# Two sixteen-head attentions: the values as stationary blocks, the denominators summed on GpSimd

## What is computed

```python
def _L0_xattn_ref(q, k, v, mask, Wq, bq, Wk, bk, Wv, bv, Wo, bo):
    B, N, DIM, H = (2, 512, 256, 16)
    qh = _split_heads(q @ Wq.T + bq)
    kh = _split_heads(k @ Wk.T + bk)
    vh = _split_heads(v @ Wv.T + bv)
    attn = jnp.einsum('bhqc,bhkc->bhqk', qh, kh) * SCALE
    attn = jnp.where(mask == 0, -jnp.inf, attn)
    attn = jax.nn.softmax(attn, axis=-1)
    out = jnp.einsum('bhqk,bhkc->bhqc', attn, vh)
    ...
    return out @ Wo.T + bo
...
x = x + jnp.tanh(g_xattn[0]) * _L0_xattn_ref(_layernorm(x, axis=-1), ctx_1024, ctx_1024, mask_1x1xSxS2_ik0, ...)
x = x + jnp.tanh(g_ffn[0]) * _L0_ffn_ref(_layernorm(x, axis=-1), ...)
...
x = x + jnp.tanh(g_xattn[3]) * _L3_xattn_ref(_layernorm(x, axis=-1), ctx_1024, ctx_1024, ...)
x = x + jnp.tanh(g_ffn[3]) * _L3_ffn_ref(_layernorm(x, axis=-1), ...)
```

## Time and profile before

| | us |
|---|---|
| median of three runs | 1044.92 (1043.39 to 1045.66) |
| the profiled execution's own time, its span | 1043.2 |
| first attention, its loop | about 29.4 to 139.5 |
| second attention, its loop | about 686.7 to 792.2 |
| TensorE busy over the span | 964.7 (92%) |
| VectorE busy | 603.3 (58%) |
| ScalarE busy | 489.0 (47%) |
| GpSimd busy | 287.8 (28%) |

### The profile page before, as it was taken

How to read it: one execution, slowest core, us unless ns; L and a number is a source line. 1 busy time by engine, 2 the same in 40 slices (tenths; PEclk the granted TensorE clock), 3 DMA queues, 4 the chain that set the end, 5 groups by cost and what they waited for, 6 DMA issues and landing times. The chain is left out here.

```text
span 1043.2 us, 18151 instructions
## 1 busy us (share of the span) xinstructions
PE 964.7 (92%) x6476; PEld 835.3 (80%) x6477; DVE 603.3 (58%) x1253; ACT 489.0 (47%) x744; POOL 287.8 (28%) x271
## 2 busy tenths in 40 slices
PE   6999999989999999877988889999998999999997
PEld 5778878878888888565777778887885799999996
DVE  5858769951223222689898999666776522222221
ACT  3654422111111111688785878255552556656561
POOL 2000000033444442280006112600000344444442
PEclk9999999999999999998999999999999999999999
DMA  9200040025667664011000010260115223322332
GB/s 295 69 1 22 21 143 21 21 77 166 181 181 210 182 168 91 15 41 41 1 1 2 1 41 2 99 231 21 41 42 171 83 45 50 48 45 48 51 45 31
DMA packets 62500, 79.38 MB, mean 76 GB/s; under 512 B 7340, under 2 KB 46855, under 8 KB 62439
## 3 DMA queue, kind: packets, MB, share of 16 engines
q1 hardware_dynamic: 48807, 59.95, 17.0%
q0 software_dynamic: 13632, 18.62, 10.2%
HBM read 60.73 MB, written 17.83 MB: 75 GB/s over the span
## 5 line engine op out<-in xcount | busy, mean ns | idle before, releaser
L3165 PEld LDWEIGHTS ps<-room,xn_sb 128*128 128x128 f32 x1248 | 145.6, 192 | 2.7 <-issue 0.8
L3165 PE MATMUL ps<-room,xn_sb 128*128 128x128 f32 x1248 | 146.3, 275 | 0.6 <-issue 0.6
L288 POOL TENSOR_TENSOR norm_vec<-norm_vec,powers 128x4 f32<-128x4 f32 (+2 forms) x27 | 28.9, 1071 | 360.7 <-DVE norm_vec L282 360.7
L3118 POOL DMA_INDIRECT out_x<-f_yo,f_give x39 | 62.0, 1589 | 110.5 <-DVE f_yo L3363 97.5
L3234 ACT ACTIVATE xn_sb<-w_L_ffn_w 128x1024 f32 x78 | 82.1, 1057 | 20.8 <-DVE f_te L3331 10.8
L3357 DVE TENSOR_TENSOR room<-room,ps 128x512 f32<-128x512 f32 x39 | 26.8, 687 | 109.5 <-PE ps L3165 109.5
L2857 DVE TENSOR_TENSOR room<-room,ps 128x1024 f32<-128x1024 f32 x24 | 29.3, 1219 | 104.0 <-issue 89.5
L2461 PE MATMUL ps<-b_room,room 128*128 128x256 f32 x384 | 85.6, 380 | 3.7 <-DVE room L2857 1.6
L2461 PEld LDWEIGHTS ps<-b_room,room 128*128 128x128 f32 x384 | 72.6, 190 | 14.1 <-issue 1.8
L2673 ACT ACTIVATE room<-ps 128x1024 f32<-128x1024 f32 x24 | 24.6, 1023 | 115.2 <-PE ps L2441 115.2
L2418 POOL DMA_INDIRECT acc_rows<-f_eo,f_idx x32 | 52.4, 1637 | 94.7 <-DVE f_eo L2883 50.9
(11 more groups left out here) (404 smaller groups left out, 2059.4 us busy)
## 6 DMA issues: line engine op xcount, KB each, us to landing
w_L_ffn_w<-in_L_ffn_w SPq DMA_DIRECT2D x24, 512.0 KB, 9.8
b_room<-in_L_ffn_Wg SPq DMA_DIRECT2D x16, 512.0 KB
b_room<-in_L_ffn_Wu SPq DMA_DIRECT2D x16, 512.0 KB
b_room<-in_L_ffn_Wd SPq DMA_DIRECT2D x16, 512.0 KB, 6.3
xn_rows<-xn_sb SPq DMA_DIRECT2D x8, 512.0 KB, 2.9
x_sb<-in_x SPq DMA_DIRECT2D x4, 512.0 KB, 6.4
xn_sb<-in_L_ffn_w SPq DMA_DIRECT2D x2, 1024.0 KB, 7.6
x_sb<-acc_rows SPq DMA_DIRECT2D x4, 512.0 KB, 5.9
```

The source lines that it names most:

```text
L3118: pool.indirect_dma_start(out_rows[:, :], bass.IndirectOffsetOnAxis(ap=give[:, j:j + 1], axis=0), yo[j % 2][:, :], None, compute_op=ALU.ad ...
L3165: m = pe.matmul(ps[:, banks[p], f * P:(f + 1) * P], wb[p][:, n, i, f * P:(f + 1) * P], xsT[p][:, i * P:(i + 1) * P], start=(i == 0), stop= ...
```

## The change

The heads are padded from 77 to 80 keys in the probabilities, so that 16 heads are 1280 columns, ten whole blocks, five for each half of the heads.

- `values`: the value blocks (128 keys x 32 columns, two heads) are stationary, the transposed probabilities move, 128 columns. Sixteen matmuls write four column groups of 32 columns each, first with the blocks of the two full rounds (early), then with the last round (late). What comes out is the output already transposed, so `turn_heads` and its copy on ScalarE are gone.
- Denominators: no column of ones is left in the value blocks. `denominators(n)` on GpSimd adds the exponentials 640, 320 and 160 wide; `inverse(n)` on VectorE, at the head of tile n, reduces the remaining 160 columns to 16 and takes the reciprocal; `widen(n)` on ScalarE spreads it over 256 columns, ahead of the tile's probability copies; TensorE transposes these two blocks in the third round; `normalise` is one multiply of the PSUM output by them.
- The third round is one copy of 512 columns: two blocks of probabilities and two of inverses.
- `project(n-1)` moves from the end of the tile to the place of `turn_heads`.
- `add_bias` moves from VectorE to GpSimd, behind the denominators.
- GpSimd's roots for the feed-forward are issued one by one inside the loop, a cast of lane numbers moves behind the loop, twenty selects of the opening become two. `place_values` has five matmuls in place of ten.

The core of the diff:

```diff
                     m.then_inc(s_ready, 1)
 
                 def turn(n, which):
+
                     pe.wait_ge(p_ready, n + 1)
                     for r in which:
-                        lo, hi = rounds[r]
                         if r == 2:
                             pe.wait_ge(pt_sb, 3 * n + 1)
-                        elif n:
-                            pe.wait_ge(pt_sb, 3 * n)
-                        for part in range(lo, hi):
-                            w = rows[part]
-                            m = pe.transpose(ps[0:w, 4 + r % 2, (part - lo) * P:(part - lo + 1) * P],
-                                             pr[:, n % 2, part * P:part * P + w], K.ident[:, :])
+                            for half in range(2):
+                                lo = half * HALF + 4 * P
+                                pe.transpose(ps[:, 4, half * P:(half + 1) * P], pr[:, n % 2, lo:lo + P], K.ident[:, :])
+                            pe.wait_ge(r_wide, n + 1)
+                            for k in range(KT):
+                                m = pe.transpose(ps[:, 4, (2 + k) * P:(3 + k) * P], wide[:, k * P:(k + 1) * P], K.ident[:, :])
+                        else:
+                            if n:
+                                pe.wait_ge(pt_sb, 3 * n)
+                            for q in range(4):
+                                lo = r * HALF + q * P
+                                m = pe.transpose(ps[:, 4 + r, q * P:(q + 1) * P], pr[:, n % 2, lo:lo + P], K.ident[:, :])
                         m.then_inc(pt_ps, 1)
 
                 def values(n):
+
+                    b = n // TB
                     if n:
-                        pe.wait_ge(on_ready, n)
-                    for r, (lo, hi) in enumerate(rounds):
-                        pe.wait_ge(pt_sb, 3 * n + r + 1)
-                        for part in range(lo, hi):
-                            w, h = rows[part], head0[part]
-                            m = pe.matmul(ps[:, 6, h * HV:(h + 3) * HV], pT[0:w, n % 2, part, :],
-                                          vblk[0:w, n // TB, part, :, :].rearrange("p j c -> p (j c)"),
-                                          start=(part == 0), stop=(part == NC - 1), skip_group_check=True)
+                        pe.wait_ge(oT_sb, n)
+                    for late in range(2):
+                        for half in range(2):
+                            pe.wait_ge(pt_sb, 3 * n + (3 if late else half + 1))
+                            for i in range(4):
+                                q = i + late
+                                m = pe.matmul(ps[i * RG:(i + 1) * RG, 6, half * P:(half + 1) * P],
+                                              vblk[:, q, 2 * b + half, 0 if late or i == 0 else 1, :], pT[:, n % 2, half if q < 4 else 2, q if q < 4 else half, :],
+                                              start=(half == 0 and not late), stop=bool(late), skip_group_check=True)
                     m.then_inc(o_ready, 1)
-
-                def turn_heads(n):
-                    pe.wait_ge(on_ready, n + 1)
-                    if n:
-                        pe.wait_ge(x_done, n)
-                    for k in range(KT):
-                        m = pe.transpose(ps[:, 7, k * P:(k + 1) * P], on[:, n % 2, k * P:(k + 1) * P], K.ident[:, :])
-                    m.then_inc(oT_ps, 1)
 
                 def project(n):
                     pe.wait_ge(oT_sb, n + 1)
                     if n == 0 and bo is not None:
                         pe.wait_ge(s_gbo, 1)
+                    if n:
+                        pe.wait_ge(x_done, n)
                     for k in range(KT):
-                        m = pe.matmul(ps[:, 7, D:2 * D], oT[:, k * P:(k + 1) * P], wo[:, k, :],
+                        m = pe.matmul(ps[:, 7, 0:D], oT[:, n % 2, k * P:(k + 1) * P], wo[:, k, :],
                                       start=(k == 0), stop=(k == KT - 1))
                     m.then_inc(y_ready, 1)
 
...
                         pe.wait_ge(q_sb, 4 * KT)
                     turn(n, (0, 1))
                     if n:
-                        turn_heads(n - 1)
+                        project(n - 1)
                     else:
                         scores(2)
-                        pe.wait_ge(s_vblk, 3)
+                        pe.wait_ge(s_vblk, PARTS + 1)
                         if bo is not None:
                             pe.wait_ge(*rest_in)
...
                         turn_second(n)
                     if ahead is not None:
                         ahead.tensor(pe, n, s_used)
-                    if n:
-                        project(n - 1)
-                unread(pe, K, 5, 2)
-                turn_heads(NT - 1)
-                unread(pe, K, 5, 1)
+                unread(pe, K, 5, 3)
                 project(NT - 1)
                 if ahead is not None:
                     ahead.tensor_end(pe)
...
                     act.wait_ge(p_in, n + 1)
                     if n >= 2:
                         act.wait_ge(pt_ps, 3 * (n - 1))
-                    act.activation(pr[:, n % 2, :], sm[:, n % 2, :], ACT.Exp).then_inc(p_ready, 1)
+                        act.wait_ge(s_den, 3 * (n - 2) + 1)
+                    act.activation(pr[:, n % 2, :].rearrange("p (h k) -> p h k", h=H)[:, :, 0:L],
+                                   sm[:, n % 2, :].rearrange("p (h k) -> p h k", h=H), ACT.Exp).then_inc(p_ready, 1)
+
+                def widen(n):
+
+                    act.wait_ge(r_den, n + 1)
+                    if n:
+                        act.wait_ge(pt_ps, 3 * n)
+                    act.activation(wide[:, :].rearrange("p (h d) -> p h d", h=H),
+                                   rden[:, n % 2, :].unsqueeze(2).broadcast_to([P, H, HD]), ACT.Copy).then_inc(r_wide, 1)
 
                 def copy_values():
                     act.wait_ge(s_vc, 1)
...
                     if n == TB - 2:
                         copy_queries(1, 0, (0, 1))
                         copy_queries(1, 1, (2, 3))
-                    for r, (lo, hi) in enumerate(rounds):
-                        if n and r == 2:
-                            act.wait_ge(oT_ps, n)
-                            act.activation(oT[:, :], ps[:, 7, 0:D], ACT.Copy).then_inc(oT_sb, 1)
+                    widen(n)
+                    for r in range(3):
                         act.wait_ge(pt_ps, 3 * n + r + 1)
                         if n >= 2 and r == 0:
                             act.wait_ge(o_ready, n - 1)
-                        if r < 2:
-                            act.activation(pT[:, n % 2, lo:hi, :].rearrange("p a b -> p (a b)"),
-                                           ps[:, 4 + r, :], ACT.Copy).then_inc(pt_sb, 1)
-                        else:
-                            act.activation(pT[:, n % 2, lo, :], ps[:, 4, 0:P], ACT.Copy)
-                            act.activation(pT[0:rows[-1], n % 2, lo + 1, :], ps[0:rows[-1], 4, P:2 * P],
-                                           ACT.Copy).then_inc(pt_sb, 1)
+                        if n >= 2 and r == 2:
+                            act.wait_ge(oT_sb, n - 1)
+                        act.activation(pT[:, n % 2, r, :, :].rearrange("p a b -> p (a b)"),
+                                       ps[:, 4 + r % 2, :], ACT.Copy).then_inc(pt_sb, 1)
                     if n in SECOND:
                         copy_second(n)
                     if n == 0:
...
+                def denominators(n):
+
+                    def add(src, w):
+                        lo = H * (LP - 2 * w)
+                        to = sm[:, n % 2, lo:lo + H * w].rearrange("p (h k) -> p h k", h=H)
+                        pool.tensor_tensor(to, src[:, :, 0:w], src[:, :, w:2 * w], ALU.add).then_inc(s_den, 1)
+                        return to
+
+                    pool.wait_ge(p_ready, n + 1)
+                    forty = add(pr[:, n % 2, :].rearrange("p (h k) -> p h k", h=H), LP // 2)
+                    pool.wait_ge(s_den, 3 * n + 1)
+                    twenty = add(forty, LP // 4)
+                    pool.wait_ge(s_den, 3 * n + 2)
+                    add(twenty, LP // 8)
+
+                def add_bias(n):
+                    if n == 0:
+                        pool.wait_ge(s_gbo, 2)
+                    elif n == 4:
+                        pool.wait_ge(norm.by_act, 4)
+                    elif n == TB:
+                        pool.wait_ge(norm.by_act, NT - 4)
+                    pool.tensor_tensor(K.x[:, n, :], K.x[:, n, :], gbo[:, :], ALU.add).then_inc(s_bias, 1)
+
+                if first:
...
                     dve.wait_ge(p_in, n + 1)
                     dve.sem_inc(s_used, 1)
 
+                def inverse(n):
+
+                    lo = H * (LP - LP // 4)
+                    dve.wait_ge(s_den, 3 * n + 3)
+                    dve.tensor_reduce(den[:, n % 2, :], sm[:, n % 2, lo:lo + H * LP // 8].rearrange("p (h k) -> p h k", h=H), AX.X,
+                                      ALU.add).then_inc(s_sum, 1)
```

(29 more changed lines are left out.)

130 lines of the change are left out of this document (69 added, 61 removed).

## The result

The changed kernel takes 1055.73 us (median of 4 runs, 1054.41 to 1056.91), beside 1045.01 for the kernel before in the same set of runs: a ratio of 1.010, 95% interval 1.0082 to 1.0118. It is 10.7 us slower; 1044.5 was forecast, with a range up to 1060 and a chance of 0.43 for slower. The time lies inside the range, but well outside the forecast's own 1040 to 1050, and the case that happened is none of those that were priced.

The account below looks back on a forecast made before the run. TensorE was taken as the bound, VectorE 0.5 us behind. Terms -1.15 + 1.35 - 1.6 - 1.2 + 3.0 - 0.8 = -0.4 took 1044.9 to 1044.5 us; range 1036 to 1060, the forecast's own 1040 to 1050.

Parts of the forecast that it names:

- What bounds the kernel now, and what TensorE gives back: Attention tiles: TensorE sets the pace, VectorE 0.5 us behind; values fall from 2.17 to 1.0 us.
- The rivals on that: Column groups in values: tile-shape switches cost +5 us, 1050, chance 0.07; groups do not overlap, +35, 1080, chance 0.04.
- The values cycle: Chain from inverse through widen, copies, transposes and values to multiply: 5.88 us per tile with rows; -1.15 first attention, +1.35 second.
- chain hidden: Faster rival: VectorE's front covers the chain from inverse to values, rows tiles take 5.77 us; 1037.5, chance 0.24.
- GpSimd: Denominator adds 2.8 us and bias 0.63 on GpSimd, 3.4 in a tile of 5.9; nothing waits for them: zero.
- The rival on GpSimd: Slower rival: GpSimd's adds double to 6.8 us a first-attention tile and become the bound past 5.9; 1058.5, chance 0.07.
- The last tiles and the end: Tiles 14 and 15 lengthen by 0.77 and 1.66 us, the end saves 0.9: net +1.5 an attention, +3.0.
- The turns: Turning tiles 7, 8, 11, 12 of the first attention go from 6.49 to 6.08 us; turns of tiles 1 to 4 unchanged.
- Project moved: Project no longer covers ScalarE's copy of the turns; turning tiles give -1.6 us in the first attention, -1.2 in the second.
- Prologue: Placing the values takes 2.0 us at most after 2.2 before; taken as -0.4 each, -0.8, bounds 0 and -1.
- The cast: GpSimd's moved cast of lane numbers lies beside other work: zero, at worst 2 us at the end.
- The clock: Slower rival: TensorE, busy 4.6 of 5.9 us, falls to 1.2 GHz; 1058 in ten tiles, over 1150 in all; chance 0.13.

Follow-up runs that it names:

- hold_wmid: `hold` with ScalarE's widen moved between the first and second copy of probabilities: 1037.89 us, ratio 0.9932 to the kernel before.
- hold: The changed kernel with GpSimd's adds of a tile waiting for the inverse of the tile before: 1042.05 us, ratio 0.9975 to the kernel before.
- hold_pend: `hold` with the project of tile n-1 back at the end of TensorE's tile: 1068.02 us, ratio 1.0227 to the kernel before.
- lanes: The changed kernel with GpSimd's cast of lane numbers back ahead of the second attention's loop: 1056.44 us, ratio 1.0118 to the kernel before.
- all_cast: The changed kernel with rows on ScalarE and widen between the first two copies, the cast left behind the loop: 1030.89 us.
- rows_act: The changed kernel with rows normalised by ScalarE, a shift for them computed on VectorE: 1037.30 us, ratio 0.9925 to the kernel before.
- hold_bias: `hold` with the output bias back on VectorE, ahead of the multiply: 1047.22 us, ratio 1.0008 to the kernel before.

## Why the prediction was wrong

*What bounds the kernel now, and what TensorE gives back*: right. The values take 1.08 us where nothing interrupts them (32 records at 76.13), 1.0 with a tail of 0.17 was said; the column groups overlap, and no cost of a switch shows. The rivals on that fall.

*The values cycle*: right, in its place and its size. Once the adds are kept away, tiles with rows take 5.84, for 5.88 by the sum, and the last intervals 5.83 and 6.66, for 5.88 and 6.77; widen starts 0.32 ahead of the copy (0.31), the inverse takes 0.52 (0.61). The rival "chain hidden" falls, and `hold_wmid` shows what a shorter chain gives: 4 us.

*GpSimd*, the step that failed: "so nothing waits for them: zero". The adds' own time was well sized (2.8 said, 3.06 measured with the gaps between them; bias 0.63 and 0.73), and nothing does wait for their result. The step looked for a wait by semaphore and for a slower GpSimd, and the bounds, one add or two, were both put on GpSimd. What it left out is VectorE as the one that is held. The row it leaned on, L301 at 1212 ns or 2420 (1212 is the shortest, the median is 1215), was read as GpSimd's loss, and it has the mirror image here, GpSimd's adds steady at 1533 to 1566 ns and VectorE's rows at 0.4 to 1.6 us. Its own trace held both: of the eight operations of that row, those from 651.26 to 657.79 us take 1.8 to 2.4 us beside VectorE's operations on two inputs (lines 1501 and 1509), two of which take 0.85 and 0.89 in place of 0.69; the other five take 1.21, most of them beside residuals and statistics.

The missing term is 1.4 us in each of five tiles with rows of an attention. Two of the ten pairs, ahead of the queries of tile 6, are hidden (VectorE's front waits there over 5 us in any case, and the interval is 14.19 in the changed kernel and 14.20 in `hold`): 8 x 1.4 = 11.2. `hold` measures 13.7. From residual to residual the profiles tell the rest: three of the eight tiles, which no stretch at the lower clock touches, are 1.26, 1.48 and 1.43 longer than in `hold`; the other five, with the tile behind one of them, are 9.2 longer together, and 5 x 1.4 is 7.0. So some 2.2 stand where the granted clock was 0.50.

The rival on GpSimd thus had the engine and the place, but the wrong victim and a wrong point from which it decides: not GpSimd's tile passing 5.9, but any meeting of an add with a row.

The Trainium skill had been quoted on it (GPSIMD Engine Reference, Specifications), and was read too narrowly: its sentence names instructions in a two-port mode beside those with two SBUF inputs, and only the second half was looked for in the tile. The Trainium skill (SBUF — State Buffer, SBUF: two separate sides) says it in full: the pair of ports is an exclusive lock, held for the whole instruction, and the other fully blocks. The trace agrees: a row ends 0.15 behind an add, a shift of two elements 0.01 behind a cast of 1.89. That the rows run in such a mode, no run here shows.

*The last tiles and the end*: right, +0.72 and +1.50 in the first attention of `hold`, and -0.91 at its end, for +0.77, +1.66 and -0.9.

*The turns.* Turning tiles take 6.26 in the first attention of `hold`, 6.08 was said. The turns of tiles 1 to 4, "I take as unchanged", are a mis-sized term: their intervals from front to front fall by 1.4 in the first attention and by 2.2 in the second. In the profiles each attention of `hold` is 3.0 shorter than before, from first front to last residual, 6.0 where the sum had -0.4, and these turns are 3.6 of it. The stage of the cast takes 2.3 of that back and the stages behind it 2.1, so that `hold` comes to -2.7. That it lies near the sum is luck.

*Project moved.* The prediction counted the cover that is lost. That the residual no longer waits for the project stands in its sum without a price; by `hold_pend` it is worth 26 us.

*Prologue.* The -0.4 each is right, 2.15 to 1.74 from the first placing matmul to what follows, but the prediction's own prices, 2.2 and 2.0, give -0.2. The gate's matmuls, its price for a step, are also not the only column-tiled ones of the trace (line 2477 has eight, line 1874 four); nothing else hangs on that.

*The cast*, "zero, at worst 2 us at the end": the stage takes 9.6 to 10.7 in the profiles that have it there and 7.2 to 7.7 in the others. The medians of `lanes` and `all_cast` do not show it, and that stays open.

*The clock*, given 0.13: the case as it was priced, a TensorE that falls because it is busy 4.6 us of 5.9, did not come. In `hold` TensorE is busy 4.97 us of a tile of 5.83, as long as in the changed kernel's 7.10, and the granted clock is 1.00 there and throughout its loops:

```profile
97.25:103.08 5.83, 4.97 (x73) 3.63 (x69) 5.23 (x9) 2.94 (x6) 3.69 (x5) 1.00 0.01 3
```

Three of the four falls in the changed kernel's loops stand behind waits for a copy that hung on held rows, the fourth stands behind a wait of 2.09 us for the scores of tile 8, up to 739.16. `hold` has that wait as well, 2.05 and 2.09, without a fall; in `rows_act` and `hold_wmid`, whose rows are not held, the clock fell to 0.50 behind it, from 79.3 us on. What decides, these runs do not show.

Of the chances, slower had 0.43 and came by a case outside the list. That the range held is luck: its upper end was there for the clock and for a GpSimd that becomes the bound, and neither made this time.

## What to carry to other kernels

That nothing waits for its result does not make element work on GpSimd free. Look which VectorE operations run at that moment, and whether they read and write SBUF; which of those are held has to be measured. Price both directions, GpSimd held by VectorE and VectorE held by GpSimd, and place the GpSimd work beside VectorE's steps on PSUM, or put the SBUF steps on ScalarE. When one engine is relieved, add up the chain that takes over; here that sum was good to 0.1 us, and the term that failed stood beside it.

## What was not expected of the hardware

VectorE's held operations did not grow by a factor, they ended with GpSimd's: a row of 0.41 us took up to 1.63, and an operation of 0.16 on two elements took 1.83 beside a cast of 1.89. Not every operation is held: the statistics, one input from SBUF, took 0.43 beside an add as without it, and so did the residual, one input from SBUF and one from PSUM, 0.47. The bias on VectorE, two inputs from SBUF, took 0.57 in place of 0.43 where it began during the last add of `hold_bias`, and that add took 0.58 to 0.63 in place of 0.49 where it began during a bias: here the loss fell on either engine. Which property of the row normalisation makes it one of the held ones, these runs do not tell apart.
